# Two graph layers in one kernel: the last source batches of layer two as 3, 2, 1, 1 tiles in the place of 2, 2, 2, 1

## What is computed

```
edge_index = stack([src, dst])
h = maximum(layernorm(x), 0)
# layer 1: h_all[r] = h @ weight[r].T ; messages of edge e are h_all[type[e], src[e]]
x = x + segment_sum(h_all[edge_type, src], dst) + bias
h = maximum(layernorm(x), 0)
# layer 2: loops are added; norm = rsqrt(deg)[src] * rsqrt(deg)[dst]
x = x + leaky_relu(segment_sum(norm * (h @ W)[src], dst) + b, 0.2)
```

## Time and profile before

| | us |
|---|---|
| median of 3 runs | 2232.4 (2232.18 to 2233.9) |
| profiled execution | 2232.29 |
| its span, first to last instruction | 2228.1 |
| PE busy | 1941.2 (87%) |
| DVE busy | 1249.4 (56%) |
| ACT busy | 1578.3 (71%) |
| POOL busy | 1619.2 (73%) |

### The profile page before, as it was taken

How to read it: one execution, slowest core, us unless ns; L and a number is a source line. 1 busy time by engine, 2 the same in 40 slices (tenths; PEclk the granted TensorE clock), 3 DMA queues, 4 the chain that set the end, 5 groups by cost and what they waited for, 6 DMA issues and landing times.

```text
span 2228.1 us, 43485 instructions
## 1 busy us (share of the span) xinstructions
PE 1941.2 (87%) x14027; PEld 1770.0 (79%) x14027; DVE 1249.4 (56%) x3564; ACT 1578.3 (71%) x3885; POOL 1619.2 (73%) x1719
## 2 busy tenths in 40 slices
PE   1567878788888899778989999999999999999998
PEld 1466777777787788768878889998999999998887
DVE  7467567557667766855776642332332333544468
ACT  6646677678787778767887886777676867776640
POOL 2777777777777777777777777777777777777726
PEclk9888998989999899999999999999999999999999
DMA  9535456455655655565666586565565555665658
GB/s 299 161 110 149 145 164 186 145 151 182 185 174 176 203 170 151 170 182 156 188 204 200 157 259 201 165 191 166 151 169 160 161 158 154 173 153 140 153 107 113
DMA packets 339332, 377.89 MB, mean 170 GB/s; under 512 B 219427, under 2 KB 256548, under 8 KB 338980
## 3 DMA queue, kind: packets, MB, share of 16 engines
q0 software_dynamic: 85312, 221.42, 35.6%
q1 hardware_dynamic: 236772, 110.05, 18.3%
q10 hardware_dynamic: 17024, 43.63, 5.5%
HBM read 299.78 MB, written 75.19 MB: 168 GB/s over the span
## 4 chain that ended last, share of the span: by engine, by line
PE 55%; POOL 20%; issue 9%; ACT 6%; DMA 4%; DVE 3%; SPq 0%; DVEq 0%; ACTq 0%; POOLq 0%
POOL rows_f L1125 19%; PE ps_slot L1642 19%; PE ps_slot L1704 13%; PE ps_proj L1658 11%; PE ps_aux L1704 9%; PE ps_slot L1672 3%; DMA rows_f<-table,idxT 3%; ACT gap_f L1353 2%; DMA abuf_f<-counts_d 1%; ACT staged_f L1303 1%; ACT wide_f L1346 1%; POOL recs_f L1113 1%; ACT onehot_f L1361 1%; DVE hots_f L1534 1%; DVE acc_f L1572 1%
## 5 line engine op out<-in xcount | busy, mean ns | idle before, releaser
L1125 POOL DMA_INDIRECT rows_f<-table,idxT x1612 | 1532.3, 951 | 491.4 <-issue 477.3
L1642 PE MATMUL ps_slot<-onehot_f,rows_f 128*128 128x128 f32 x6448 | 873.1, 288 | 154.7 <-DMA rows_f<-table,idxT 135.6
L1642 PEld LDWEIGHTS ps_slot<-onehot_f,rows_f 128*128 128x128 f32 x6448 | 827.3, 201 | 186.3 <-DMA rows_f<-table,idxT 149.8
L1353 ACT ACTIVATE gap_f<-iota,keyT 128x128 bf16<-128x128 bf16 x1614 | 528.9, 399 | 8.7 <-PEq L141 2.8
L1303 ACT ACTIVATE staged_f<-ps_slot 128x392 uint8<-128x392 f32 x784 | 335.1, 500 | 209.4 <-PE ps_slot L1672 209.0
L1531 DVE TENSOR_TENSOR hots_f<-ps_slot,keys_f 128x392 bf16<-128x392 bf16 x784 | 276.9, 353 | 272.9 <-PE ps_slot L1672 271.6
L1361 ACT ACTIVATE onehot_f<-gap_f 128x384 f32<-128x384 bf16 x538 | 279.7, 520 | 134.0 <-PE ps_slot L1642 133.8
L1658 PE MATMUL ps_proj<-w0t,acc_f 128*128 128x256 f32 x1568 | 357.1, 381 | 1.4 <-DVE acc_f L1436 1.4
L1436 DVE TENSOR_TENSOR acc_f<-ps_slot,acc_f 128x256 f32 x538 | 227.0, 422 | 185.3 <-PE ps_slot L1642 125.0
L1534 DVE TENSOR_TENSOR hots_f<-ps_slot,keys_f 128x512 bf16<-128x512 bf16 x784 | 324.1, 413 | 0.1
L1704 PE MATMUL ps_slot<-wide_f,stash_f 128*128 128x512 f32 (+1 forms) x1336 | 323.0, 385 | 1.3 <-issue 1.3
(11 more groups left out here) (164 smaller groups left out, 863.6 us busy)
## 6 DMA issues: line engine op xcount, KB each, us to landing
counts_d<-staged_f ACTq DMA_DIRECT2D x98, 392.0 KB
rows_f<-table,idxT POOLq DMA_INDIRECT x1612
abuf_f<-counts_d SPq DMA_DIRECT2D x57, 320.0 KB
stash_f<-table SPq DMA_DIRECT2D x14, 1280.0 KB, 7.8
table<-hs_f SPq DMA_DIRECT2D x48, 256.0 KB
xt_f<-in_x_dram SPq DMA_DIRECT2D x48, 128.0 KB
out_dram<-xt_f SPq DMA_DIRECT2D x48, 128.0 KB
xres<-in_x_dram SPq DMA_DIRECT2D x9, 640.0 KB, 13.5
```

The lines of the kernel that those rows point to most:

```text
L1125: eng.indirect_dma_start(rows0[:, k, c, :], None, V["table0"], bass.IndirectOffsetOnAxis(ap=idxT[:, n * LOT + c:n * LOT + c + 1], axis=0)) ...
L1353: last = eng.activation(gap[:, n % 2, c, :], iota[:, :], ACT.Abs, scale=-1.0, bias=V["key"][:, n * LOT + c:n * LOT + c + 1])
L1642: last = eng.matmul(o[:, b * W:(b + 1) * W], rows0[:, k, c, b * P:(b + 1) * P], onehot[:, n % HOTS, c, :], start=(c == 0), stop=(c == chun ...
```

## The change

One number row of the planner is another one. The source batches 10 to 12 are now tiles 42 to 44, tiles 45 and 46, tile 47.

```diff
-BATCHES = (5, 5, 5, 5, 5, 5, 5, 3, 2, 2, 2, 2, 2, 1)
+BATCHES = (5, 5, 5, 5, 5, 5, 5, 3, 2, 2, 3, 2, 1, 1)
```

## The result

The changed kernel takes 2243.4 us (median of 4 runs, 2242.16 to 2243.83), the kernel before, on the same chip, 2233.2 (4 runs, 2232.18 to 2235.21): 1.0046 times the time, 95% interval 1.0034 to 1.0059. The forecast was 2242.8. The profiled execution took 2243.29 us, where that of before took 2232.29: 11.0 us more.

A forecast was written before the change was run, and what follows sets the result against it. PE bounds it up to project 48, with POOL's gathers as floor, then DVE. Project 48 6.5 us late (5.0 pieces, 1.5 clock) plus 4.0 tail gives 10.5 us over 2232.3: forecast 2242.8, range 2236.0 to 2248.5.

The forecast's parts named there:

- the clock's term: PE, lots 532 and on: a half-clock spell begun at about 2104 has 3 us left, delaying project 48 by 1.5 us.
- The floor of lot 532: PE, caught up, starts lot 532 when its rows come: 3.0 us behind its last gather's start at 2111.44, so 2114.4.
- the room: PE, lots 529 to 531: no dense work gives 7.2 us; entering about 2 us late leaves 5.2 us.
- Lots 532 to 537: PE's lots, project 47 and 11 two-tile pieces take 23.75 us, so project 48 starts at 2138.15, 5.0 us late.
- Rival 2: The clock stays low: the 13.7 us spell begins at lot 532, costing 6.8 us, not 1.5; 2248.1 us; chance 0.17.
- The last output takes 4.9 us behind DVE as now: Program's end: the last output's time behind DVE stays 4.9 us, so the change adds nothing there.
- The tail: Behind project 48: 7.9 us of adds, less 5.2 of waits filled, plus 1.5 behind PE's slower pieces; 4.0 us taken.
- rival 3: PE, not DVE's adds, sets the tail; batch 11's pieces fill two stops, 2.3 us less; 2230 us; chance 0.06.
- rival 1: Only the tail counts: PE reaches project 48 as now; 2236.3 us; chance 0.10.
- The two stops in the seam: PE's stops of 1.05 and 1.26 us get filled, but lie where DVE is late, so counted 0.
- rival 4: DVE's adds in a row cost full duration, 0.69 and 0.55 us start to start; 3.4 us more, 2246.2; chance 0.04.
- rival 5: Count loads landing in over 5 us make batch 12's units wait, 2 us in all; 2245 us; chance 0.04.

The follow-up runs named there:

- Batch 11 held: Changed kernel with tiles 45 and 46 not allowed ahead of project 48; 2247.6 us, ratio to before 1.0063, and 1.0039 on the slow chip.
- the pair at the end: Kernel before with last batches 42 and 43, 44, 45, 46, then 47 and 48 together; 2228.1 us, ratio 0.9980; second time 2229.1 us, 0.9981.
- Three single tiles: Kernel before with tiles 46, 47 and 48 as a batch each, 46 held from coming ahead of project 48; 2243.3 us, ratio 1.0043.
- narrow adds: Changed kernel with the 26 adds of batch 12 (tile 47) cut to one column, all matmuls kept; 2238.3 us, ratio to before 1.0022.
- the first experiment: Changed kernel with no piece behind lot 537: three pieces between the last lot and project 48 go behind it; 2242.8 us, ratio to before 1.0043.
- the smaller pair at the end: Kernel before with last batches 42 and 43, 44 and 45, 46, then 47 and 48; 2232.8 us, ratio 0.9996, and 0.9991 on the slow chip.

## Why the prediction was right, point by point

The time was 0.6 us off, but that is partly luck: in the profiled execution the clock's term was 1.5 us too much, and against it stand 0.6 us of gathers, 0.3 in the tail and 1.1 in the program's end, which were not in the sum. So the steps are worth more than the sum.

*The floor of lot 532.* 3.0 us behind its last gather's start was taken, 2.89 measured (2112.04 to 2114.93). PE stood caught up as the step said, with stops of 1.41, 1.25 and 0.44 us on lots 530 to 532. But the room was 3.1 us and not the 5.2 that the step had reckoned, so the margin was smaller than it looked.

*Lots 532 to 537.* 23.75 us summed, 23.80 measured. Since the order had nothing but lots, project 47 and 11 pieces in it, counting them at row prices was enough. Batch 11 held confirms it from the other side: without the pieces project 48 starts at 2133.54.

*The clock: wrong.* The step that failed took 1.5 us for half clock on lots 532 and on, from the premise "Lots 529 to 531 leave PE as idle as then". They did not: PE stopped for 3.1 us in three stops, none over 1.41, where it had stopped for 9.1 us in four from 2054 to 2073. (That the clock stayed up for this reason isn't shown.) In the profiled execution the clock was 1.00 from 2036.58 to 2231.14, and 0.50 only from 2022.93 to 2026.34 and from 2033.17 to 2036.58, where PE does lots, stops for gathers and one half of a project (4.62 us in the place of 3.46); the stops at lots 530 to 532 took that up. The term measured 0. The spell does come there in another kernel (2108.56 to 2115.39 in the pair at the end, where PE stopped for 3.29 us ahead of it, and where it cost lot 532 1.2 us), so the risk was real, its place right, and the value for this kernel wrong. Rival 2 is out here.

*Not in the sum.* The last gathers were 0.6 us later in this execution, and nothing in the change is known to do it. With this and the clock the start of project 48 was 2138.73, forecast 2139.6; without the 1.5 the steps give 2138.15, and with the 0.6 they give 2138.75. "The last output takes 4.9 us behind DVE as now" holds for the work and not for the time: the time lay 9.05 us behind DVE's end before and 10.16 after, for the reason in the last section.

*The tail.* 4.0 us forecast, 4.26 measured. The order of its parts is as told: gaps of up to 0.21 us while pieces have two tiles, the last at 2159.3, and no gap after. The first add of one tile starts 13.9 us behind the end of project 48 (2145.80 to 2159.73), where the sum had 13.5; a stop of PE of 0.35 us at 2150.72 is most of that. From there DVE takes 73.4 us to its end, where the sum had 73.3. Three single tiles gives the price of the adds alone, and narrow adds shows which of the two engines is the bound for pieces of one tile; rival 3 falls with them, and rival 1 with the start of project 48 in the changed kernel and with batch 11 held. The two stops in the seam were called worth 0; the one ahead of project 48 was in the sum all the same, since the 5.0 us are counted from a start, 2133.11, that contained it: the first experiment brings it back.

*Adds at full duration (rival 4).* Three adds of 512 columns start 0.60 us apart in the tail after the change too (2159.73 to 2161.53). The Trainium skill, VectorE: DVE Perf Modes, section "The TRN2 errata — SBUF-src ops pay a fixed extra latency per instruction", gives 691 ns for one; that agrees with the 0.69 of the add alone at 2148.17, and not with a row of them. The rows' price was the right one.

*Loads of counts (rival 5).* Out for the time, but closer than thought. ACT's waits for loads of counts from 2134 to 2240 us in the changed kernel (total, times, longest):

```profile
ACT wide_f L1346 <- DMA abuf_f<-counts_d: 2.1, 5, 0.6
ACT wide_f L1346 <- DMA keys_f<-counts_d: 1.8, 1, 1.8
```

With one more of 0.6 us (`acc_f`) these are 4.5 us in all. DVE had no gap in batch 12, so they cost no time; that ACT's ring of 8 covers them is the likely reason, and wasn't tested.

*The experiment with no piece behind lot 537* was expected to bring project 48 forward by 2.8 us and brought 1.1: its expectation forgot that the pieces had covered the stop of 1.05 us in the earlier trace rows, the same which the prediction had set at 0. Of the rest, 0.4 us is the later last lot.

## What to carry to other kernels

Where a stream of small products ends in a tail, price each piece there by the slower of its two engines: the matmul grows with the sources in it, the add to the sum does not, so a batch of one source made DVE the bound (0.60 against 0.46 us) and a batch of two made PE (0.91). What counts is then how many pieces are left when the last serial step (here project 48) is over; a piece moved ahead of it costs less, and nothing at all where it fills a stop, so the last batch should hold two late sources and those before it should be small enough to be done in time. Find first the floor below which nothing ahead can move (here POOL's gathers): stops above it are free, and adding them up as a loss misleads.

## What the runs showed of the hardware

**One chip was 20% slower, and why isn't shown.** There the kernel before took 2674 us. POOL's gathers, first on that chip (the smaller pair at the end), then on a usual one (batch 11 held); count, then busy us, mean ns, then idle ahead of them by what ended it:

```profile
L1125 POOL DMA_INDIRECT rows_f<-table,idxT x1612 | 1535.7, 953 | 896.8 <-issue 401.8 <-remote 258.3 <-PE ps_slot L1642 236.7
```

```profile
L1126 POOL DMA_INDIRECT rows_f<-table,idxT x1612 | 1532.3, 951 | 491.3 <-issue 474.5 <-PE ps_slot L1643 16.8
```

A gather lasts as long (953 against 951 ns), and POOL is idle for longer, but so are others: ACT waits 202 us for "remote" ahead of one of its copies too. "Remote" is what the profile writes where it finds no instruction of this core or known queue that ended a wait; it is no proof of another core. By the chain of waits it isn't the gathers that hold this chip up. The chain's shares of the span on that chip, then in the kernel before on a usual one:

```profile
PE 57%; issue 14%; ACT 10%; another core or an unknown queue 8%; DVE 7%; DMA 1%; DVEq 1%; POOL 0%; ACTq 0%; SPq 0%
PE 55%; POOL 20%; issue 9%; ACT 6%; DMA 4%; DVE 3%; SPq 0%; DVEq 0%; ACTq 0%; POOLq 0%
```

POOL falls from 20% to nothing, and 8% stand at what the profile can't name. The ratios to the kernel before agree between such a chip and a usual one for the smaller pair (0.9991 and 0.9996), and hardly for batch 11 held (1.0039 and 1.0063, with intervals that just overlap), so comparisons are made here only within one chip.

**Short stops did not always halve TensorE's clock.** Stops of 1.41, 1.25 and 0.44 us on lots 530 to 532 left it at 2.4 GHz in the changed kernel. In the pair at the end, second run, it was at 1.2 GHz from 2108.11 to 2114.93 about a stop of 2.36 us for a gather:

```profile
2107.68 2.56 PE L1642 MATMUL ps_slot<-onehot_f,rows_f 128*128 128x128 f32 x12 [2.36 <-DMA rows_f<-table,idxT]
2111.32 4.66 PE L1642 MATMUL ps_slot<-onehot_f,rows_f 128*128 128x128 f32 x24 [1.09 <-DMA rows_f<-table,idxT]
```

These lots take 2.3 to 2.6 us each where they take 1.60 at the higher level. The stops ahead of the fall were longer than those of the changed kernel at this place, but the length of one stop doesn't decide it. In the kernel before, the stop of 2.25 us in the earlier trace rows has the fall right behind it, at 2054.43, and this one, longer, has none (the clock is 1.00 from 2068.09 on):

```profile
2073.11 1.60 PE L1642 MATMUL ps_slot<-onehot_f,rows_f 128*128 128x128 f32 x12 [2.42 <-DMA rows_f<-table,idxT]
```

What decides it isn't shown by these runs. Whether a spell cost anything depended on whether PE stood idle in it or behind it anyway.

**A span can end in something that is no work, and the time with it.** The span of the changed kernel's profiled execution is 13.3 us longer than before's (2241.4 against 2228.1), its time 11.0 and DVE's end 9.9. The last instruction is a branch in PE's program. It starts 4.5 us behind DVE's end in both, so the output takes as long. Count, shortest, median and longest ns, and start, before and then changed:

```profile
L503 PEldq COMPARE_BRANCH  x1: 422/422/422, 2227.7 to 2227.7; - x1
L503 PEldq COMPARE_BRANCH  x1: 3834/3834/3834, 2237.6 to 2237.6; - x1
```

Where this branch lasts 0.4 us (before, no piece behind lot 537, narrow adds, batch 11 held, and the pair at the end the first time) the time lies 8.8 to 9.2 us behind DVE's end; where it lasts 3.6 to 4.0 (changed, three single tiles, both executions of the smaller step, and the pair at the end the second time) 10.0 to 10.4. The pair at the end is one kernel with both, so this differs from one execution to the next and isn't work of a change; what it is stays open. The four executions of the changed kernel have their times 1.8 to 1.9 us above their spans, as goes with the long branch, and those of the kernel before, timed beside the experiments, have either kind, so up to 1.1 of the 10.2 us between the medians may be this. The end of the last instruction of compute is the better mark when a few microseconds are looked for.
